# Attention with two heads stacked in the row halves of the TensorE array, maxima over two PSUM banks, one value bank, and V kept in SBUF

## The chip, the cores and the metric

The kernel runs on 1 core of one Trainium2 chip. The metric is device time in microseconds for one launch. TensorE is called PE, VectorE DVE, ScalarE ACT, GpSimd POOL and SyncE SP, as the profile does.

## The reference

Two pre-norm layers on x of shape (2, 1024, 256), fp32. Only the first step is touched by the change:

```
qkv   = layernorm(x) @ W_attn                      # 16 heads; q1,k1,q2,k2 of 8 columns a head, v of 16
attn  = q1 k1^T * scale - lam * q2 k2^T * scale    # per head, 1024 x 1024
out   = (1 - LAMBDA_INIT) * softmax(attn) @ v ;  x = x + out @ W_proj
x = x + sparse ternary MLP(layernorm(x)) ; x = x + linear attention(...) ; x = x + routed MLP(...)
```

Since q2 is scaled by -lam, a head's score is one product of contraction 16. There are 2 batches x 16 heads = 32 score matrices of 1024 x 1024.

## The kernel before, in words

Work is cut into 8 groups of G = 4 heads. Operands are split into a high fp32r part and a low rest, and a head's q and k are stacked over partitions: `qst` holds (q_hi, q_lo, q_hi), `kst` (k_hi, k_hi, k_lo), 48 rows, then two rows that hold minus the row maximum in q (high and low part) and ones in k. Rows 50 to 127 are zero in q, so that each product uses all 128 rows of the array. Each of the three ring buffers has 4 heads side by side, [128, 4, 1024].

`stage_qkv` (L157) computes q, k and v for four chunks of 512 tokens. SP writes q and k parts to DRAM (L233), v rows padded to 32 columns a head (L237), and after the second chunk loads the stack of group 0 (L244). POOL clears stacks and v buffers first. SP's instructions are in the order of the code, and the stage ends when every engine is done.

`stage_attention` (L440) has three kinds of work:
- max units (`side_unit`, L572): one 128 x 512 tile of q k^T for the maxima; 64 tiles a group, into a ring of 3 banks `ps_m`. DVE reduces each (L710), and after the last one of a group `finish_max` (L699 to L704) makes the two rows of negated maxima, which SP copies into `qst` with 8 small DMAs (L535).
- score units (`score_unit`, L592): the transposed tile k q^T with the maxima subtracted, into a ring of 3 banks `ps_s`; ACT takes the exponential (L684) into `prob`.
- value units (`value_unit`, L605): four fp32 products, one a head, each in its own 32 columns of the array, accumulate into `ps_o`, which has two banks, one for each half of the queries. The compiler makes two matmul instructions of one fp32 product, so one unit is 8 matmuls of 512 columns. After a group ACT copies `ps_o` (L691), PE transposes it (L578) and DVE divides by the sum of the exponentials (L720 to L723).

PE runs an order written out by hand: max and score alternate tile by tile, and after every 4 tiles of each there is one value unit. The maxima of group g+1 are made beside the scores of group g, with the last one 7 units (14 score tiles) ahead of the scores that need it (`LEAD`). Ahead of the first scores stands a prologue of 76 max tiles, into which the ternary weights of the MLP are worked: their sum (L614) after tile 34, their transposes (L631) at tiles 64 to 67 and 71 to 74, with L526 loading the weights, L546 to L554 on POOL, L675 on ACT. Before the stage's loads, SP waits for the writes of q, k and v (L523).

## Time and profile before

| | us |
|---|---|
| median of 3 runs (lowest, highest) | 1344.59 (1342.28, 1345.54) |
| profiled execution, span | 1344.7 |
| PE / DVE / ACT / POOL busy | 1139.2 / 921.8 / 630.1 / 231.4 |
| granted TensorE clock, mean | 0.911 of full speed |
| first max tile on PE | 89.72 |
| first exponential | 140.16 |
| first instruction of the next stage | 532.66 |

Times inside the profile are microseconds from the span's start. A group of instructions has a busy time and a mean duration of one; consecutive instructions of one engine overlap, so that the distance from start to start is shorter than the mean. Matmul ends are modelled. "Idle before" is the time the engine waited ahead of these instructions, with what ended most of it.

### The profile page before, as it was taken

The page shows a single profiled execution, that of the slowest core. Times are in us where ns is not written, and L with a number is a line of the kernel's source. Part 1 is how long each engine was busy: PE and PEld are TensorE (multiplying, and loading weights), DVE is VectorE, ACT ScalarE, POOL GpSimd, SP SyncE. Part 2 cuts the span into 40 slices and gives each one's busy share as a digit, 9 for nine tenths or more (in the row PEclk, how much of TensorE's full clock was granted, in tenths as well). Part 3 has the DMA queues.
Part 4 walks back from the last instruction along what each step waited for, and adds up shares of the span by engine and source line. Part 5 has one row for each costly group of instructions (what it writes and reads, how often), then busy time and mean ns, then how long its engine had stood idle before and what let it go on. Part 6 is the DMA issues. An engine that isn't in the chain of part 4 may idle for free. (4 is left out here: it accounts for less than half of the span.)

```text
span 1344.7 us, 16323 instructions
## 1 busy us (share of the span) xinstructions
PE 1139.2 (85%) x5920; PEld 820.3 (61%) x5920; DVE 921.8 (69%) x1953; ACT 630.1 (47%) x1106; POOL 231.4 (17%) x178
## 2 busy tenths in 40 slices
PE   0959999999999998655575747999999799999888
PEld 0834555555555533544464635888887589889786
DVE  8739888888888820458988867555554677777743
ACT  2413766676666676267664213333333433433233
POOL 9006300000000000100003322100000644744200
PEclk9965999999999999777787878999999899999859
DMA  2794422421431000000000020100000000000200
GB/s 87 213 287 66 65 33 34 64 41 26 64 39 28 1 2 32 4 1 0 1 1 1 1 82 1 48 17 32 33 16 0 32 1 1 1 1 1 83 0 4
DMA packets 34221, 48.55 MB, mean 36 GB/s; under 512 B 5310, under 2 KB 22218, under 8 KB 34122
## 3 DMA queue, kind: packets, MB, share of 16 engines
q1 hardware_dynamic: 34140, 47.51, 16.0%
q8 instruction: 47, 0.77, 0.2%
q14 instruction: 34, 0.28, 0.1%
HBM read 32.52 MB, written 14.71 MB: 35 GB/s over the span
## 5 line engine op out<-in xcount | busy, mean ns | idle before, releaser
L710 DVE TENSOR_REDUCE att_mx<-att_ps_m 128x1 f32<-128x512 f32 x512 | 316.3, 681 | 66.8 <-PE att_ps_m L572 66.8
L684 ACT ACTIVATE att_prob<-att_ps_s 128x512 f32<-128x512 f32 x512 | 267.2, 604 | 115.6 <-PE att_ps_s L592 115.5
L572 PE MATMUL att_ps_m<-kst,qst 128*128 128x512 f32 x512 | 227.5, 468 | 18.5 <-PEq L74 16.0
L592 PE MATMUL att_ps_s<-qst,kst 128*128 128x512 f32 x512 | 200.7, 404 | 4.9 <-ACT att_prob L684 4.7
L572 PEld LDWEIGHTS att_ps_m<-kst,qst 128*128 128x128 f32 x512 | 102.3, 200 | 142.2 <-DVE att_mx L710 111.0
L1719 POOL TENSOR_TENSOR qry_prod<-qry_qr,lin_ksum 128x512 f32<-128x512 f32 x64 | 87.9, 1375 | 307.3 <-ACT qry_qr L1786 307.3
L605 PE MATMUL att_ps_o<-att_prob,att_vst 128*32 128x512 f32 x1024 | 136.2, 604 | 0.0
L592 PEld LDWEIGHTS att_ps_s<-qst,kst 128*128 128x128 f32 x512 | 94.8, 188 | 42.3 <-ACT att_prob L684 27.8
L1786 ACT ACTIVATE qry_qr<-qry_ps_q 128x512 f32<-128x512 f32 x64 | 38.3, 598 | 129.8 <-PE qry_ps_q L152 116.4
L1462 DVE SCALAR_TENSOR_TENSOR key_k_lo<-key_ps_k,key_k_hi 128x512 fp32r<-128x512 f32 x64 | 44.2, 690 | 67.8 <-ACT key_k_hi L1542 67.3
L1103 ACT ACTIVATE mlp_junk<-mlp_z,mlp_nlev 128x1024 bf16<-128x1024 f32 x64 | 72.6, 1137 | 23.2 <-DVE mlp_nlev L939 21.6
L152 PE MATMUL qry_ps_o<-qry_m_hi,qry_n_hi 128*128 128x256 f32 x256 | 76.5, 299 | 0.9 <-DVE qry_n_lo L1749 0.8
L152 PE MATMUL qry_ps_o<-qry_m_lo,qry_n_hi 128*128 128x256 f32 x256 | 71.0, 277 | 0.0
L152 PE MATMUL qry_ps_o<-qry_m_hi,qry_n_lo 128*128 128x256 f32 x256 | 70.9, 277 | 0.0
L1749 DVE TENSOR_TENSOR qry_n_lo<-qry_ps_t,qry_n_hi 128x512 fp32r<-128x512 f32 x64 | 44.2, 691 | 37.3 <-ACT qry_n_hi L1775 36.9
L1542 ACT ACTIVATE key_k_hi<-key_ps_k 128x512 fp32r<-128x512 f32 x64 | 38.2, 597 | 66.0 <-PE key_ps_k L152 65.3
L829 POOL CAST mlp_wo_t<-ternary 128x2048 f32<-128x2048 bf16 x1 | 1.9, 1891 | 386.4 <-POOLq L508 386.4
L152 PE MATMUL key_ps_k<-key_w_hi,lin_xt_hi 128*128 128x512 f32 x128 | 54.2, 424 | 1.7 <-DVE lin_xt_lo L1421 1.7
L1739 DVE SCALAR_TENSOR_TENSOR qry_qn<-qry_rec,qry_qr 128x512 f32<-128x512 f32 x64 | 53.5, 836 | 2.2
L152 PE MATMUL qry_ps_q<-qry_w_hi,lin_xt_hi 128*128 128x512 f32 x128 | 51.7, 404 | 3.3 <-DVE qry_w_lo L1759 3.3
L152 PE MATMUL qry_ps_q<-qry_w_lo,lin_xt_hi 128*128 128x512 f32 x128 | 51.5, 402 | 0.0
L152 PE MATMUL key_ps_g<-key_k_hi,key_xk_hi 128*128 128x512 f32 x128 | 50.5, 395 | 0.6 <-DVE key_k_lo L1462 0.6
(348 smaller groups left out, 2395.6 us busy)
## 6 DMA issues: line engine op xcount, KB each, us to landing
qst<-qk_parts SPq DMA_DIRECT2D x24, 256.0 KB
kst<-qk_parts SPq DMA_DIRECT2D x24, 256.0 KB
qk_parts<-att_out SPq DMA_DIRECT2D x16, 256.0 KB, 3.3
qk_parts<-qkv_qk_lo SPq DMA_DIRECT2D x16, 256.0 KB, 3.4
att_vst<-v_rows SPq DMA_DIRECT2D x8, 512.0 KB
residual<-L_attn_x SPq DMA_DIRECT2D x4, 512.0 KB, 5.7
v_rows<-qkv_v_st SPq DMA_DIRECT2D x8, 256.0 KB, 5.4
v_rows<-ternary SPq DMA_DIRECT2D x8, 256.0 KB, 4.0
```

The lines of the kernel that those rows point to most:

```text
L152: ins = nc.tensor.matmul(out, a, b, start=first and n == 0, stop=last and n == len(terms) - 1)
L572: nc.tensor.matmul(ps_m[:, n % BANKS, :], qst[g % RING][:, h, t * P:(t + 1) * P], kst[g % RING][:, h, half * d.CH:(half + 1) * d.CH], star ...
L592: nc.tensor.matmul(ps_s[:, n % BANKS, :], kst[g % RING][:, h, s * P:(s + 1) * P], qst[g % RING][:, h, t * d.CH:(t + 1) * d.CH], start=True ...
L605: ins = nc.tensor.matmul(ps_o[32 * h:32 * h + 32, t, :], vst[g % RING][:, s, 32 * h:32 * h + 32], prob[:, n % RING, h, t * d.CH:(t + 1) * ...
L684: nc.scalar.activation(prob[:, s % RING, h, t * d.CH:(t + 1) * d.CH], ps_s[:, n % BANKS, :], ACT.Exp).then_inc(exp_ok, 1)
L710: nc.vector.reduce_max(mx[:, g % 2, m // NB, m % NB:m % NB + 1], ps_m[:, n % BANKS, :], AX.X)\
L1103: nc.scalar.activation(junk[:, n % 2, :], Z[:, t, :], ACT.Sign, bias=nlev[:, t:t + 1], accum_out=sgn[:, t:t + 1]).then_inc(cnt_ok, 1)
L1462: nc.vector.scalar_tensor_tensor(out=k_lo[:, i % 2, :], in0=ps_k[:, i % 2, :], scalar=0.0, in1=as_f32(k_hi[:, i % 2, :]), op0=ALU.max, op1 ...
L1719: nc.gpsimd.tensor_tensor(prod[:, u % 2, :], qr[:, u % 2, :], ksum[:, b, cols(n)], ALU.mult).then_inc(pr_ok, 1)
L1739: nc.vector.scalar_tensor_tensor(out=qn[:, u % 2, :].rearrange("p (h e) -> p h e", e=HW), in0=rec[:].unsqueeze(2).to_broadcast([P, HPB, HW ...
L1749: nc.vector.tensor_tensor(n_lo[:, u % 2, :], ps_t[:, u % 2, :], as_f32(n_hi[:, u % 2, :]), ALU.subtract).then_inc(n_ok, 1)
L1786: nc.scalar.activation(qr[:, u % 2, :], ps_q[:, u % 2, :], ACT.Relu).then_inc(q_ok, 1)
```

## The change

- `qst` and `kst` hold two heads in two row halves: head 2j in rows 0 to 49, head 2j+1 in rows 64 to 113, [128, 2, 1024]. Each product uses 50 (maxima: 48) rows of one half. Zero rows and their DRAM copy are gone; a stack is loaded with 12 DMAs in place of 7, the negated maxima with 16 in place of 8.
- The two heads' products are issued one behind the other, into two banks. A max unit is such a pair, read by one DVE reduction over two banks (`ps_m` is 2 x 2 banks). Scores are issued as pairs, into the same ring of 3 banks; one wait stands before both.
- The steps go over (group, query half t, key tile s); a step has two slots, each with a score pair, then a max pair, then one half (256 columns) of the value product of two steps earlier. `ps_o` is one bank: the values of a t start in the fourth step of it, after ACT's copy of the t before; there two slots have none, and the two after them a whole value product each.
- `prob` is a ring of 6 steps of 512 queries. V stays in SBUF (`vall`); its DRAM copy and its loads are gone.
- The prologue has 42 max pairs, the sum of weights after pair 17, the transposes at 32 to 35 and 37 to 40. The last maxima of a group stand 5 steps (10 slots) ahead of its scores.

Core of the diff (longer removed passages stand in the code above):

```diff
-                sp.wait_ge(pad_ok, 1)
-                sp.dma_start(zero_dram, as_f32(qst[0][64:66]).rearrange("r h t -> r (h t)")).then_inc(z_out, 16)
...
                     if c == d.S // d.CH - 1:
-                        sp.wait_ge(z_out, 16)
+                        sp.wait_ge(pad_ok, 2 * len(kst))
                         for i in range(d.S // d.CH):
                             sp.wait_ge(qk_out[i], 32 * NQ)
                         load_stack(d, keep, scratch, 0, sp, stack_in)
...
+                link(nc.gpsimd.memset(vall[:], 0.0))
+                nc.gpsimd.memset(vall[:, :, :, d.HD:d.HD + 1], 1.0).then_inc(v_init, 1)
+                pool.wait_ge(v_init, 1)
+                for i in range(2 * len(kst)):
+                    rows = slice(ROW2 * (i % 2) + 32, ROW2 * (i % 2) + 64)
+                    nc.gpsimd.memset(as_f32(kst[i // 2][rows, :, :]), 1.0).then_inc(pad_ok, 1)
...
-STACK_LOADS = 7
+STACK_LOADS = 12
+ROW2 = 64
...
+            src = scratch["qk"][part, b, base + h0 * d.HD:base + (h0 + d.G) * d.HD, :]\
+                .rearrange("(j r e) t -> r e j t", r=2, e=d.HD)
+            for r in range(2):
+                row = ROW2 * r + n * d.HD
+                sp.dma_start(as_f32(dst[row:row + d.HD, :, :]), src[r]).then_inc(sem, 16)
...
+        PR = 6
+        LEAD = 5
+        LAG = 2
...
-        ps_m = st.ps("ps_m", [P, BANKS, d.CH])
-        ps_o = st.ps("ps_o", [P, NB, d.CH])
-        pad_ok, gp = st.sem("pad_ok"), st.sem("gp")
+        ps_m = st.ps("ps_m", [P, 2, 2, d.CH])
+        ps_o = st.ps("ps_o", [P, d.CH])
...
+        SPG = NS * NB
+        MPG = PAIRS * NS * NB
+        STEPS = SPG * d.NG
+        NMD = 16
+        END = STEPS + LAG + 4
+        side = {u: [] for u in range(-1, END)}
         for g in range(d.NG):
             for m in range(MPG):
-                side[max(-1, UPG * (g - 1) - LEAD + m // MPU)].append(("max", g, m))
+                side[max(-1, SPG * (g - 1) - LEAD + m // PAIRS)].append(("max", g, m))
             for t in range(NB):
-                side[UPG * (g + 1) + G + 2 + t].append(("out", g, t))
-        items = [(u, x) for u in side for x in side[u]]
+                side[NS * (NB * g + t + 1) + LAG + 2].append(("out", g, t))
+        items = [x for u in side for x in side[u]]
+        values = {}
+        for u in range(STEPS):
+            for c in range(2):
+                slot = 2 * (u + LAG) + c
+                if u % NS < 2:
+                    slot = 2 * (u // NS * NS + LAG + 1) + u % NS
+                values.setdefault(slot, []).append((u, c))
...
                 def load_group(g):
...
+                    if g >= RING:
+                        sp.wait_ge(sc_ps, PAIRS * SPG * (g - RING + 1))
+                    load_stack(d, keep, scratch, g, sp, load[g % RING])
...
-                    sp.wait_ge(scratch["v_out"][i], 16 * (d.H // d.G) * d.NC // 2)
-                load_group(0)
...
+                    for n, src in enumerate((nm_hi, nm_lo)):
+                        for r in range(2):
+                            row = ROW2 * r + 3 * HD + n
+                            dst = qst[g % RING][row:row + 1, :, :].rearrange("p h (t q j) -> p (h t) q j", q=4, j=32)
+                            for q in range(4):
+                                cols = slice(32 * q + PAIRS * NS * r, 32 * q + PAIRS * NS * (r + 1))
+                                sp.dma_start(as_f32(dst[:, :, q]), as_f32(src[cols, g % 2, :]))\
+                                    .then_inc(nm_in[g % 2], 16)
...
-                pad(nc, link, keep, RING - 1).then_inc(pad_ok, 1)
...
-                    if n >= BANKS:
-                        pe.wait_ge(m_rd, n - BANKS + 1)
+                    if n >= 2:
+                        pe.wait_ge(m_rd, n - 1)
                     if kind == "max":
-                        h, t, half = m // (NS * NB), m // NB % NS, m % NB
+                        j, t, half = m // (NS * NB), m // NB % NS, m % NB
                         if m == 0 and g:
                             pe.wait_ge(load[g % RING], loaded(g))
-                        nc.tensor.matmul(ps_m[:, n % BANKS, :], qst[g % RING][:, h, t * P:(t + 1) * P],
-                                         kst[g % RING][:, h, half * d.CH:(half + 1) * d.CH],
-                                         start=True, stop=True).then_inc(m_ps, 1)
+                        for r in range(2):
+                            rows = slice(ROW2 * r, ROW2 * r + 3 * HD)
+                            ins = nc.tensor.matmul(ps_m[:, n % 2, r, :], qst[g % RING][rows, j, t * P:(t + 1) * P],
+                                                   kst[g % RING][rows, j, half * d.CH:(half + 1) * d.CH],
+                                                   start=True, stop=True)
+                        ins.then_inc(m_ps, 1)
...
+                def score_pair(u, j):
+                    g, t, s = u // SPG, u // NS % NB, u % NS
+                    n = G * u + 2 * j
+                    if u % SPG == 0 and j == 0:
                         pe.wait_ge(nm_in[g % 2], 16 * NMD * (g // 2 + 1))
-                    if n < BANKS:
+                    if n == 0:
                         pe.wait_ge(tern_rd, 2 * TB)
                     else:
...
+                        pe.wait_ge(exp_ok, n + 2 - BANKS)
+                    for r in range(2):
+                        rows = slice(ROW2 * r, ROW2 * r + 3 * HD + 2)
+                        ins = nc.tensor.matmul(ps_s[:, (n + r) % BANKS, :], kst[g % RING][rows, j, s * P:(s + 1) * P],
+                                               qst[g % RING][rows, j, t * d.CH:(t + 1) * d.CH], start=True, stop=True)
+                    ins.then_inc(sc_ps, 1)
+                def value_half(u, c):
+                    g, t, s = u // SPG, u // NS, u % NS
+                    b, h0 = g // (d.NG // d.B), g % (d.NG // d.B) * G
+                    pe.wait_ge(exp_ok, G * (u + 1))
+                    if s == 0 and c == 0 and t:
+                        pe.wait_ge(o_rd, t)
+                    if s == 0 and c:
+                        return
+                    cols = slice(c * HALF, (c + 1) * HALF) if s else slice(0, d.CH)
                     for h in range(G):
...
+                        ins = nc.tensor.matmul(ps_o[32 * h:32 * h + 32, cols], vall[:, NS * b + s, h0 + h, :],
+                                               prob[:, u % PR, h, cols], start=s == 0,
+                                               stop=s == NS - 1 and c == 1)
+                    ins.then_inc(pv_ok, 1 if s else 2)
...
-                for u in side:
+                for u in range(END):
                     todo = side[u]
-                    for t in range(NB):
+                    for j in range(PAIRS):
+                        if u < STEPS:
+                            score_pair(u, j)
                         for x in todo[:1]:
                             side_unit(*x)
-                        if u < UN:
-                            score_unit(u, t)
                         todo = todo[1:]
+                        for v in values.get(2 * u + j, []):
+                            value_half(*v)
                     for x in todo:
                         side_unit(*x)
-                    if u > G and u % G in (1, 3) and u // G - 1 < UN // G:
-                        value_unit(u // G - 1, u % G // 2)
...
+                for u in range(END):
+                    for j in range(PAIRS if u < STEPS else 0):
+                        n = G * u + 2 * j
+                        if j == 0 and u >= PR:
+                            act.wait_ge(pv_ok, 2 * (u - PR + 1))
+                        act.wait_ge(sc_ps, PAIRS * u + j + 1)
+                        for r in range(2):
+                            nc.scalar.activation(prob[:, u % PR, 2 * j + r, :], ps_s[:, (n + r) % BANKS, :],
+                                                 ACT.Exp).then_inc(exp_ok, 1)
+                    last = u - LAG - 1
+                    if last > 0 and last % NS == NS - 1:
+                        t = last // NS
+                        act.wait_ge(pv_ok, 2 * (last + 1))
+                        if t >= NB:
+                            act.wait_ge(m_rd, place("out", t // NB - 1, t % NB))
+                        nc.scalar.activation(osb[:, t % NB, :], ps_o[:], ACT.Copy).then_inc(o_rd, 1)
...
-                        nc.vector.reduce_max(mx[:, g % 2, m // NB, m % NB:m % NB + 1], ps_m[:, n % BANKS, :], AX.X)\
-                            .then_inc(m_rd, 1)
+                        nc.vector.reduce_max(mx[:, g % 2, :, m], ps_m[:, n % 2], AX.X).then_inc(m_rd, 1)
```

## Rows read from the trace of the kernel before

**Rows 1.** The page's costliest groups: xcount | busy us, mean ns | idle before, releaser.
```profile
L710 DVE TENSOR_REDUCE att_mx<-att_ps_m 128x1 f32<-128x512 f32 x512 | 316.3, 681 | 66.8 <-PE att_ps_m L572 66.8
...
L684 ACT ACTIVATE att_prob<-att_ps_s 128x512 f32<-128x512 f32 x512 | 267.2, 604 | 115.6 <-PE att_ps_s L592 115.5
...
L605 PE MATMUL att_ps_o<-att_prob,att_vst 128*32 128x512 f32 x1024 | 136.2, 604 | 0.0
```
**Rows 2.** Windows, busy us (count) by engine, granted clock, DMA share, GB/s.
```profile
140.00:486.00 346.00, 344.54 (x1811) 177.37 (x1809) 283.88 (x499) 238.36 (x462) 6.19 (x2) 1.00 0.28 39
...
74.00:90.00 16.00, 0.28 (x1) 0.31 (x2) 0.00 (x0) 0.32 (x1) 0.21 (x1) 0.62 1.06 366
```
**Rows 3.** Timeline of PE around one value unit: start us, us, instruction, count.
```profile
301.30 0.40 PE L572 MATMUL att_ps_m<-kst,qst 128*128 128x512 f32 x1
301.53 0.40 PE L592 MATMUL att_ps_s<-qst,kst 128*128 128x512 f32 x1
301.86 1.07 PE L605 MATMUL att_ps_o<-att_prob,att_vst 128*32 128x512 f32 x8
302.86 0.50 PE L572 MATMUL att_ps_m<-kst,qst 128*128 128x512 f32 x1
303.19 0.39 PE L592 MATMUL att_ps_s<-qst,kst 128*128 128x512 f32 x1
```
**Rows 4.** Timeline of SP, two groups' negated maxima and a stack load.
```profile
227.94 2.41 SPq L535 DMA_DIRECT2D qst<-att_nm_hi  x4
...
242.52 1.25 SPq L424 DMA_DIRECT2D qst<-qk_parts  x3
...
278.04 2.42 SPq L535 DMA_DIRECT2D qst<-att_nm_hi  x4
```
**Rows 5.** The page's DMA issues: KB each, us to landing.
```profile
v_rows<-qkv_v_st SPq DMA_DIRECT2D x8, 256.0 KB, 5.4
...
qst<-att_nm_hi SPq DMA_DIRECT2D x32, 4.0 KB, 1.8
```
**Rows 6.** Timeline of DVE: the prologue's first group, then a steady stretch.
```profile
90.52 38.39 DVE L710 TENSOR_REDUCE att_mx<-att_ps_m 128x1 f32<-128x512 f32 x64 [18.35 <-PE att_ps_m L572]
...
129.44 2.55 DVE L703 CAST att_nm_hi<-att_nmt 128x32 fp32r<-128x32 f32 x1
...
176.89 0.22 DVE L699 TENSOR_REDUCE att_nm<-att_mx 128x32 f32<-128x64 f32 x1
...
177.72 2.48 DVE L710 TENSOR_REDUCE att_mx<-att_ps_m 128x1 f32<-128x512 f32 x4
...
196.02 0.26 DVE L720 RECIPROCAL att_rs<-att_ps_m 128x16 f32<-128x16 f32 x1 [0.72 <-PE att_ps_m L578]
...
196.86 1.28 DVE L710 TENSOR_REDUCE att_mx<-att_ps_m 128x1 f32<-128x512 f32 x2
```
**Rows 7.** Groups by form: DVE reading 128 x 1024 fp32.
```profile
L863 DVE TENSOR_TENSOR residual<-residual,mlp_ps_t 128x1024 f32<-128x1024 f32 x3 | 3.7, 1221 | 14.4 <-PE mlp_ps_t L1183 14.4
```
**Rows 8.** Timeline of ACT and PE in the last group, where no maxima are left.
```profile
512.78 2.06 ACT L684 ACTIVATE att_prob<-att_ps_s 128x512 f32<-128x512 f32 x4 [0.61 <-PE att_ps_s L592]
...
513.43 0.50 PE L592 MATMUL att_ps_s<-qst,kst 128*128 128x512 f32 x1 [0.28 <-ACT att_prob L684]
```
**Rows 9.** Timeline, end of stage_qkv and start of the attention.
```profile
67.22 12.30 SPq L237 DMA_DIRECT2D v_rows<-qkv_v_st  x4
...
73.72 0.60 ACT L366 ACTIVATE ternary<-qkv_ps_v 128x512 f32<-128x512 f32 x1 [0.83 <-PE qkv_ps_v L152]
...
85.66 3.19 SPq L237 DMA_DIRECT2D v_rows<-ternary  x4
```
**Rows 10.** Timeline, first exponentials, and what stands after the last ones.
```profile
140.16 2.06 ACT L684 ACTIVATE att_prob<-att_ps_s 128x512 f32<-128x512 f32 x4
...
525.94 2.06 ACT L684 ACTIVATE att_prob<-att_ps_s 128x512 f32<-128x512 f32 x4 [0.54 <-PE att_ps_s L592]
...
532.66 0.40 SPq L819 DMA_DIRECT2D mlp_wp<-L_attn_W_proj  x1
```

More of the change, by code:

```diff
@@ L638, in _ @@
                         prologue[TURN_AT[i] + k] = lambda i=i, k=k: turn_weight(i, k)
-                for n, x in enumerate(side.pop(-1)):
+                for n, x in enumerate(side[-1]):
                     side_unit(*x)
@@ L676, in _ @@
                         .then_inc(tern_rd, 1)
-                for u in range(UN + G + 3):
-                    s, h = u // G, u % G
-                    if h == 0 and RING <= s < UN // G:
-                        act.wait_ge(pv_ok, NB * (s - RING + 1))
-                    for t in range(NB if u < UN else 0):
-                        n = NB * u + t
-                        act.wait_ge(sc_ps, n + 1)
-                        nc.scalar.activation(prob[:, s % RING, h, t * d.CH:(t + 1) * d.CH], ps_s[:, n % BANKS, :],
-                                             ACT.Exp).then_inc(exp_ok, 1)
-                    if u > UPG and u % UPG in (2, 4):
-                        g, t = u // UPG - 1, u % UPG // 2 - 1
-                        act.wait_ge(pv_ok, NB * (NS * (g + 1) - 1) + t + 1)
-                        if g >= 1:
-                            act.wait_ge(m_rd, ready("out", g - 1, t))
-                        nc.scalar.activation(osb[:, t, :], ps_o[:, t, :], ACT.Copy).then_inc(o_rd, 1)
+                for u in range(END):
[14 more added lines that the diff above has]
+                        nc.scalar.activation(osb[:, t % NB, :], ps_o[:], ACT.Copy).then_inc(o_rd, 1)
             @block.vector
```

121 lines of the change are left out of this document (27 added, 94 removed).

## The prediction

> **What bounds the kernel now.** I read the page's groups first, then windows over the attention, then timelines of PE, ACT, DVE and SP inside it. The two largest groups of the page are the maxima on DVE and the exponentials on ACT, and both wait for PE: 66.8 and 115.6 us idle [rows 1]. From 140 to 486 us PE is busy 344.5 of 346 us at full clock, DVE 283.9, ACT 238.4 [rows 2]. A busy PE row alone proves little, so I add up its instructions. In the stretch of 8 alternating products the distance from start to start is 301.53 - 301.30 = 0.23 us. A value unit of 8 matmuls stands between a score at 301.53 and a max product whose weight load starts at 302.86; the product after that one starts at 303.19, so the first streamed from 302.96. The unit thus costs 302.96 - 301.53 - 0.23 = 1.20 us [rows 3]. Eight products and a unit are 8 x 0.232 + 1.20 = 3.05 us, 16 of them 48.8, and two sets of transposes bring a group to the 50.1 us that lie between two sets of negated maxima, 227.94 and 278.04 [rows 4]. So PE's order of instructions is the bound, and nothing else. In the last group no maxima are left, and the exchange with ACT binds: both engines wait there for each other in turn [rows 8]. A third bound stands ahead: from 74 to 90 us PE does nothing while the DMA engines are full (share 1.06) [rows 2], because SP stood 12.30 us in the issues of v rows at 67.22, and the last ones end at 88.85, though the compute of the stage ended at 74.3 [rows 9].
>
> **The products.** A score tile and a max tile cost PE 0.232 us each. The change issues two of them in two row halves. If they stream side by side, a pair costs what one cost. The trace has no row halves; it has column quarters: the 8 matmuls of a value unit, 604 ns each [rows 1], take 1.07 us together [rows 3], so that they run as two waves of four, 1.07 - 0.60 = 0.46 us apart. Four at once with no visible loss is the nearest row. Bounds for a pair: 0.232 (full overlap) and 0.464 (none); I take 0.24.
>
> **The value halves.** A wave of 256 columns takes half of 0.45 us. A whole unit costs 1.20, of which two waves are 0.90 and the turns between the arrangements of the array, with the first weight load laid bare, 0.30. A half then costs 0.45 + 0.30 = 0.75 us. So a slot, two tiles of each kind, costs PE 0.24 + 0.24 + 0.75 = 1.23 us. Before, two tiles of each kind and half a unit cost 0.93 + 0.60 = 1.53. The turns are the change's own price: two in each slot, before two in every second one. The Trainium skill speaks of less than full overlap: its page TensorE: Matmul & The Clock Gate (Part 3, Measured speedup vs the span model) gives a speedup of 3.07 for four row tiles of 512 columns. As an estimate by that figure a pair costs 0.232 x 4 / 3.07 = 0.30, a slot 0.13 more, and the whole would be 28 us above my sum; the second rival has the same sign, and the trace of before has no row half that could tell.
>
> **DVE.** 64 reductions of 512 columns take 38.39 us, 0.600 each from start to start [rows 6]; one alone 0.681 [rows 1]. A DVE instruction over 1024 columns takes 1.221 [rows 7], 0.54 more than the 0.681. A pair's reduction then takes 0.600 + 0.533 = 1.13 us from start to start. Bounds: 1.13 and 1.22. A group has 32, 36.3 us, and finish_max 0.83 (176.89 to 177.72) and two outputs of 0.84 (196.02 to 196.86) [rows 6], 38.8 us. That is under PE's sum below, with two buffers between.
>
> **ACT and its exchange with PE.** Four exponentials take 2.06 us, so (2.06 - 0.60) / 3 = 0.49 each, a pair 0.98. But a pair of scores may start only when the first exponential of the pair before is done, since three banks hold one pair and one tile. In the last group this exchange can be read: the exponential from 512.78 ends at 513.37, the score starts at 513.43 and takes 0.50, weight load included [rows 8]; then comes the exponential. Round: 0.60 + 0.05 + 0.50 + 0.04 = 1.19 us a slot. So PE's 1.23, the exchange's 1.19 and DVE's 1.13 lie close together: PE leads by a little, and no single edit gains more by itself.
>
> **A group.** Per half of the queries, 16 slots: 12 with a value half, 12 x 1.23 = 14.8; 2 without, at the exchange's 1.20, 2.4; 2 with a whole unit, 2 x (0.48 + 1.20) = 3.4. Transposes of an output: (50.1 - 48.8) / 2, 0.6 us. ps_o is one bank now: ACT copies it behind the exponentials of a step, 0.5 us of ACT, and the first value unit of the next half waits for it, about 0.4 us; behind that unit on PE stand the next score and max pairs. Sum 21.6, 1.35 a slot, 43.2 us a group in place of 50.1. Slots with maxima reach from step 0 to 106: 214 x 1.35 = 289 us. The remaining 42 slots have no max pair; PE needs 0.99 and the exchange 1.19, with the whole units 1.24 on average: 52 us. First to last exponential 341 us, where it was 528.0 - 140.16 = 387.8 [rows 10].
>
> **The negated maxima.** SP needs 2.41 us for the issue of four, 0.60 each [rows 4]; 16 in place of 8 would be 9.6 us, and 1.8 to landing [rows 5]. Each carries half as much: bounds 0.30 and 0.60, and I take the upper, since the issue of four stack DMAs with other shapes is no cheaper per instruction (1.25 for three). From the last max pair to the scores it feeds there are 10 slots and a value half, 14.1 us; off go the reduction and finish_max, 2.5. Left 11.6 against 11.4: just hidden, with 0.3 us a group of loss, 2 us. Behind the waiting score pair on PE stands everything. Loads of stacks (12 issues of 0.42 in place of 7) have over 25 us of room: free.
>
> **The front.** Without v rows, SP issues the last q and k parts as PE makes them, until 72.5 us; the stage ends with its compute (74.3) or with the stack of group 0. 16 writes of 256 KB leave the queue (8 from each of two buffers, one of them shown [rows 5]): 4.2 MB at the 366 GB/s of 74 to 90 us [rows 2] are 11.5 us. 89.7 - 11.5 is 78.2, the compute's end gives 74.7. I put the first max at 77, bounds 75 and 87 (SP still held up in the stack's 12 issues), in place of 89.7. POOL clears less than before, when it was no wait for the first stack. From the first max: 32 pairs x 1.13 = 36.3; finish_max 3.2, since its cast stretches to 2.55 beside POOL [rows 6]; then 16 issues and landing, 11.4; in all 50.9, and a score and ACT 0.6. First exponential at 128.5 (140.16 before), 11.7 us earlier. The weights of the MLP land earlier too, and their sum and transposes stand at nearly the same tiles, so their chain is no longer than before, when it too ended a little ahead of the first exponential. PE is at half clock there (0.62 from 74 to 90 [rows 2]); scores that begin at half clock cost some 3 us, which I add.
>
> **The sum.** 128.5 + 341 + 2 + 3 = 474.5 for the end of the last exponential, 528.0 before. What stands behind it (525.94 + 2.06 to 532.66, 4.7 us [rows 10]) has the same parts. Gain 53.5; V's loads during the attention lay beside PE and give nothing. The profiled execution of 1344.7 goes to 1291. The median of the runs is 1344.6, the same within their spread, so the forecast is 1291 us.
>
> **Rivals.** (1) The halves do not stream side by side (slower than before). Place: every pair; price 0.46 in place of 0.24, a slot 0.93 + 0.75 = 1.68, 1.71 with the rest of the sum; 214 x 1.71 + 42 x 1.27 = 419 us, and with the front 1344.7 - 11.7 + 419 - 387.8 = 1364. It decides from a pair of 0.24 + 53.5 / 428 = 0.37 us on. For it: no row half is in the trace; against it: the column quarters. Chance 0.10. (2) The second half's weight load is laid bare, once a pair behind a turn: a weight load is 302.96 - 302.86 = 0.10 us [rows 3]; or DVE's two-bank reading costs 1.22 and its bursts reach PE. A slot is 0.10 to 0.13 longer, 214 x 0.12 = 26 us, 1317. That two engines lie so close speaks for it, that four column quarters load their weights together against it. Chance 0.17. (3) The negated maxima come late, each at over 0.60 beside a stack load, or the front gains nothing: 7 x 1.5 or 10 us more, 1302. Chance 0.18. (4) The turns cost less than 0.30, the copy of ps_o is never waited for, and the clock is up by the first scores: 214 x 0.06 = 13, and 5 us of the losses above, 1273. Chance 0.10. The forecast, 0.45, with its own range 1277 to 1305.
>
> **Range and chances.** The range 1265 to 1320 leaves out the first rival and the far side of the fourth. Under 0.3% (4 us) no change can be told. Faster: all but the first rival and mishaps between, 0.88; same 0.02; slower 0.10.
>
> **What would show it.** Starts of the two matmuls of a pair within some 0.01 us, and the next pair 0.24 later (first rival: 0.46 between). Value halves with two waves 0.22 apart. DVE reductions of 1.21 mean, 1.13 from start to start. From 135 to 420 us slots of 1.35 us and 43 us between sets of negated maxima; a wait of PE for the rows of negated maxima under 1 us. The first max near 77 us, with no idle stretch after 74; the first exponential near 128.5. Wrong would be: DVE or ACT busy over 95% of that stretch (then the bound is another engine), or a sum per slot over 1.45.

## The result and the profile after

Before 1343.66 us (median of 4, 1342.28 to 1345.54), after 1307.65 us (median of 4, 1307.32 to 1309.97): ratio 0.9727, 95% interval 0.9709 to 0.9745. The profiled execution has a span of 1305.6 us and a mean granted clock of 0.885, where it was 1344.7 and 0.911. The change makes the kernel faster by 36 us; forecast were 53.5. Medians are over all executions of a kernel; ratios and intervals leave out those more than 1.5% above its fastest.

The page's groups after, as in [rows 1]:
```profile
L701 DVE TENSOR_REDUCE att_mx<-att_ps_m 128x2 f32<-128x1024 f32 x256 | 303.5, 1221 | 33.1 <-PE att_ps_m L556 31.0
L673 ACT ACTIVATE att_prob<-att_ps_s 128x512 f32<-128x512 f32 x512 | 278.2, 596 | 88.0 <-PE att_ps_s L579 79.6
L595 PE MATMUL att_ps_o<-att_prob,v_rows 128*32 128x256 f32 (+1 forms) x1920 | 171.2, 439 | 5.0 <-ACT att_osb L681 4.7
```
DVE and ACT still wait for PE. A DVE reduction over two banks takes the 1221 ns that [rows 7] gave.

PE's timeline in a steady stretch after, as [rows 3]:
```profile
299.93 0.50 PE L579 MATMUL att_ps_s<-qst,kst 50*128 50x512 f32 x2
300.27 0.40 PE L556 MATMUL att_ps_m<-kst,qst 48*128 48x512 f32 x2
300.60 0.64 PE L595 MATMUL att_ps_o<-att_prob,v_rows 128*32 128x256 f32 x8
301.17 0.50 PE L579 MATMUL att_ps_s<-qst,kst 50*128 50x512 f32 x2
```
Two products (x2) last 0.40 us together, as one did; the starts of a pair are 3 ns apart. A slot is 301.17 - 299.93 = 1.24 us; predicted were 1.23. From the start of a value half to the next product it is 0.57 us, 1.00 for a whole unit in [rows 3]; a pair stands 0.33 us ahead of the value half, as one product did there. The pair of 0.30 us, the prediction's estimate from the 3.07 that the Trainium skill gives for four row tiles (TensorE: Matmul & The Clock Gate, Part 3, Measured speedup vs the span model), did not come; the span model of the same section, the duration of one product and about 4 ns for each further tile, is what these rows show for two.

Windows after, with the columns of [rows 2] (the third figure from the end is the granted clock: 1.00 is 2.4 GHz, 0.50 is 1.2):
```profile
126.00:490.00 364.00, 337.70 (x2858) 122.11 (x2860) 269.11 (x284) 277.45 (x516) 0.00 (x0) 0.92 0.17 24
237.00:240.00 3.00, 3.00 (x32) 1.21 (x28) 2.96 (x3) 2.64 (x5) 0.00 (x0) 1.00 0.00 0
240.00:243.40 3.40, 2.43 (x22) 0.96 (x20) 3.35 (x4) 3.03 (x6) 0.00 (x0) 1.00 0.00 0
243.40:247.00 3.60, 3.47 (x16) 0.82 (x14) 2.55 (x6) 1.74 (x5) 0.00 (x0) 0.53 0.01 1
```
PE is busy 338 of 364 us, no longer all the time, and the clock is 0.92. The three short windows show one place of ten: the clock rises at 134.4 us and then falls ten times before the last group begins at 445.7. In the last group it falls twice more. PE's timeline there:
```profile
240.75 0.50 PE L579 MATMUL att_ps_s<-qst,kst 50*128 50x512 f32 x2
241.09 0.40 PE L556 MATMUL att_ps_m<-kst,qst 48*128 48x512 f32 x2
242.01 0.49 PE L579 MATMUL att_ps_s<-qst,kst 50*128 50x512 f32 x2 [0.52 <-ACT att_prob L673]
242.34 0.40 PE L556 MATMUL att_ps_m<-kst,qst 48*128 48x512 f32 x2
243.19 0.51 PE L579 MATMUL att_ps_s<-qst,kst 50*128 50x512 f32 x2 [0.45 <-ACT att_prob L673]
243.54 0.59 PE L556 MATMUL att_ps_m<-kst,qst 48*128 48x512 f32 x2
244.26 1.94 PE L595 MATMUL att_ps_o<-att_prob,v_rows 128*32 128x512 f32 x8
```
The slots at 240.75 and 242.01 are the two without a value product. PE waits 0.5 us in each, and right behind them the clock falls for 3.4 us: the whole value unit takes 1.94 us, 1.07 in [rows 3]. A half is 16 slots, measured from its first exponential to that of the next half. An undisturbed one takes 22.0 to 22.1 us, one with a drop 23.2 to 23.8 (22.7 where half of the maxima are gone). Of the 13 halves behind the first, which is partly at half clock from the start, ten have a drop; the second, the fifth and the tenth have the same two slots and none.

The front after, DVE and SP (as [rows 6] and [rows 4]):
```profile
102.30 3.90 DVE L694 CAST att_nm_hi<-att_nmt 128x32 fp32r<-128x32 f32 x1
...
106.45 5.04 SPq L518 DMA_DIRECT2D qst<-att_nm_hi  x8
111.54 5.01 SPq L518 DMA_DIRECT2D qst<-att_nm_lo  x8
```
The first reduction starts at 64.6 us (90.5 before), the first exponential at 120.7 (140.16), the last exponential at 491.8, the next stage at 496.26 (532.66). The attention from the first exponential to the end of the last is 371.7 us, 387.8 before. So 19.5 of the 36.4 us up to the next stage come from the front and 16.1 from the loop (the attention from its first exponential on); predicted were 11.7 and 42 (47 less the 5 us of losses set apart).

### The profile page after: what moved, and what is told of

Same layout as the page of the kernel before. It is cut to its first block and busy times, and to the rows that moved or that the text cites. A ratio compares the mean times of both kernels' runs of the same rounds, so it can differ in the third digit from the quotient of the medians.

```text
span 1305.6 us, 18000 instructions
## 1 busy us (share of the span) xinstructions
PE 1093.7 (84%) x6816; PEld 746.8 (57%) x6816; DVE 901.1 (69%) x1697; ACT 640.8 (49%) x1106; POOL 203.4 (16%) x170
## 5 line engine op out<-in xcount | busy, mean ns | idle before, releaser
L701 DVE TENSOR_REDUCE att_mx<-att_ps_m 128x2 f32<-128x1024 f32 x256 | 303.5, 1221 | 33.1 <-PE att_ps_m L556 31.0
L673 ACT ACTIVATE att_prob<-att_ps_s 128x512 f32<-128x512 f32 x512 | 278.2, 596 | 88.0 <-PE att_ps_s L579 79.6
L595 PE MATMUL att_ps_o<-att_prob,v_rows 128*32 128x256 f32 (+1 forms) x1920 | 171.2, 439 | 5.0 <-ACT att_osb L681 4.7
L579 PE MATMUL att_ps_s<-qst,kst 50*128 50x512 f32 x512 | 133.6, 518 | 21.9 <-ACT att_prob L673 20.2
L556 PE MATMUL att_ps_m<-kst,qst 48*128 48x512 f32 x512 | 123.7, 480 | 16.7 <-DVE att_mx L701 14.4
L579 PEld LDWEIGHTS att_ps_s<-qst,kst 50*128 50x128 f32 x512 | 50.3, 192 | 145.0 <-ACT att_prob L673 128.6
L1776 ACT ACTIVATE qry_qr<-qry_ps_q 128x512 f32<-128x512 f32 x64 | 38.2, 597 | 129.9 <-PE qry_ps_q L152 116.5
L595 PEld LDWEIGHTS att_ps_o<-att_prob,v_rows 128*32 128x32 f32 x1920 | 42.0, 112 | 88.0 <-ACT att_prob L673 57.4
L1093 ACT ACTIVATE mlp_junk<-mlp_z,mlp_nlev 128x1024 bf16<-128x1024 f32 x64 | 72.6, 1137 | 23.3 <-DVE mlp_nlev L929 21.8
L556 PEld LDWEIGHTS att_ps_m<-kst,qst 48*128 48x128 f32 x512 | 54.9, 211 | 44.6 <-DVE att_mx L701 36.1
L1729 DVE SCALAR_TENSOR_TENSOR qry_qn<-qry_rec,qry_qr 128x512 f32<-128x512 f32 x64 | 53.5, 836 | 2.2
L710 DVE RECIPROCAL att_rs<-att_ps_m 128x16 f32<-128x16 f32 x16 | 4.1, 257 | 72.7 <-PE att_ps_m L563 72.7
```

The costliest lines, as they stand in the source:

```text
L556: ins = nc.tensor.matmul(ps_m[:, n % 2, r, :], qst[g % RING][rows, j, t * P:(t + 1) * P], kst[g % RING][rows, j, half * d.CH:(half + 1) * ...
L579: ins = nc.tensor.matmul(ps_s[:, (n + r) % BANKS, :], kst[g % RING][rows, j, s * P:(s + 1) * P], qst[g % RING][rows, j, t * d.CH:(t + 1) * ...
L595: ins = nc.tensor.matmul(ps_o[32 * h:32 * h + 32, cols], vall[:, NS * b + s, h0 + h, :], prob[:, u % PR, h, cols], start=s == 0, stop=s == ...
L673: nc.scalar.activation(prob[:, u % PR, 2 * j + r, :], ps_s[:, (n + r) % BANKS, :], ACT.Exp).then_inc(exp_ok, 1)
L701: nc.vector.reduce_max(mx[:, g % 2, :, m], ps_m[:, n % 2], AX.X).then_inc(m_rd, 1)
L1093: nc.scalar.activation(junk[:, n % 2, :], Z[:, t, :], ACT.Sign, bias=nlev[:, t:t + 1], accum_out=sgn[:, t:t + 1]).then_inc(cnt_ok, 1)
```

## The experiments

All ratios are to the kernel before, on the same chip. The runs were on several chips, so "less than after" compares medians or ratios, not executions side by side. Times of slots are from start to start of ACT's exponentials; "first to last" is from the first exponential to the end of the last. Traces show one execution each.

### e1_fill: does the clock fall because PE has too little to do in the thin slots?

```diff
-                        for r in range(2):
+                        for r in list(range(2)) * times:
...
-                            side_unit(*x)
+                            side_unit(*x, times=1 if values.get(2 * u + j) else 3)
```

> In the slots that have no value products, each max pair is issued three times over (the same result in the same banks). Theory: the granted clock falls to half for some 3.4 us in 11 of 13 half groups because PE is thinly used in the two slots without values; then the drops between 140 and 430 us vanish, every half group takes the 22.0 us that the undisturbed ones take now, and the whole is 15 to 20 us shorter, about 1290. The last group has no max pairs and keeps its drops: 24 and 21 us a half. Rival: the drops have another cause (the row halves themselves, or their phase is accidental); then they stay and the time is the same, or up to 3 us longer for the added products. Control: the slots 4 and 5 stay at 1.19 and 1.45 us, since PE has 0.6 us to spare in them.

1292.54 us, 0.9596 (0.9576 to 0.9615): 15 us less than after, though PE does more. (Three executions took 1290.4 to 1294.3; a fourth took 1465.0 at a mean granted clock of 0.697, and no trace shows why.) Window of e1_fill:
```profile
126.20:430.00 303.80, 295.30 (x2688) 116.69 (x2684) 266.89 (x279) 245.09 (x456) 0.00 (x0) 1.00 0.20 29
```
No drop is left in it; its halves take 21.8 to 22.3 us. From the first exponential to the last group it is 308.5 us, 325.0 in the kernel after: 16.5 less, of which 2.4 lie in the first half, where the clock rose at 126.2 us in place of 134.4, and 14.1 in the ten drops. (The expectation counts eleven.) In the last group, where no maxima are left to be repeated, the clock still falls (25.1 and 23.2 us a half), which serves as a control. So with more work for PE in the two slots the clock does not fall here. That such slots are not enough by themselves is shown by the three spared halves after, and by e4_whole_values below.

### e2_same_half: both products of a pair in one row half

```diff
-                            rows = slice(ROW2 * r, ROW2 * r + 3 * HD)
+                            rows = slice(0, 3 * HD)
```

> Both products of each pair, maxima and scores, read rows 0 to 47 (49), so both stand in the same row half; the second head's scores are then those of the first. Theory (the halves stream side by side and this is what pays): the second product starts 0.23 us after the first, a regular slot goes from 1.24 to 1.70 us, the last group's from 1.19 to 1.42, and the whole is 80 to 95 us longer, about 1390, slower than the kernel before. Rival (the gain comes from fewer, longer instructions, and the exchange with ACT hides the pair's streaming): under 25 us longer.

1685.2 us, ratio 1.253. Window, and PE's timeline, of e2_same_half:
```profile
300.00:800.00 500.00, 500.00 (x1949) 225.29 (x1949) 202.25 (x205) 187.14 (x346) 0.00 (x0) 0.50 0.09 14
```
```profile
500.00 1.22 PE L579 MATMUL att_ps_s<-qst,kst 50*128 50x512 f32 x2
501.02 1.05 PE L556 MATMUL att_ps_m<-kst,qst 48*128 48x512 f32 x2
502.00 1.08 PE L595 MATMUL att_ps_o<-att_prob,v_rows 128*32 128x256 f32 x8
```
The products now run one after the other, but the clock stays at 0.50 with PE busy all the time. That was not foreseen (expected were about 1390 us), and so the run does not give the price of overlap alone. e9_all_rows was made for that.

### e9_all_rows: the pairs use all 128 rows and cannot overlap

The rows of the other head and the padding are included in each product; the row of ones is zero and the exponential is scaled, so the values are others.

```diff
-                            rows = slice(ROW2 * r, ROW2 * r + 3 * HD)
+                            rows = slice(0, P)
```

> Every product of a pair uses all 128 rows, so the two stand one behind the other, in the same number and order of instructions; the spare rows of q are cleared first, the row of ones is zero and the exponential is scaled to nothing, so the scores are not the reference's. Theory (the row halves stream side by side, at full clock): a regular slot takes 1.70 us in place of 1.24, the clock doesn't fall since the array is used whole, a half group takes 28 to 29 us, and the whole is 75 to 95 us longer, about 1390. Rival (row halves gave little, the order and the reductions gave the most): under 30 us longer, at the kernel before or below.

1373.73 us, 1.0211 (1.0186 to 1.0236). Window and PE's timeline of e9_all_rows:
```profile
127.60:500.00 372.40, 364.79 (x2496) 182.18 (x2495) 274.79 (x279) 237.62 (x442) 0.00 (x0) 1.00 0.17 24
```
```profile
300.89 0.72 PE L582 MATMUL att_ps_s<-qst,kst 128*128 128x512 f32 x2
301.46 0.63 PE L559 MATMUL att_ps_m<-kst,qst 128*128 128x512 f32 x2
```
A pair lasts 0.63 us in place of 0.40: 0.23 more, one whole product. Slots are 1.63 and 1.75 us in turn, 1.69 on average, and a half 27.9. The whole is 65 us more than after by the ratios, less than the 75 to 95 expected; in the last group the clock falls once, for 3.4 us, where the kernel after has 13.6 us at half clock. This is the first rival in the flesh (it gave slots of 1.71 and 19 us over the kernel before; here it is 28): without overlap the change would have been slower than the kernel before.

### e3_one_bank_max: two reductions of one bank each

```diff
-                        nc.vector.reduce_max(mx[:, g % 2, :, m], ps_m[:, n % 2], AX.X).then_inc(m_rd, 1)
+                        for r in range(2):
+                            ins = nc.vector.reduce_max(mx[:, g % 2, r, m:m + 1], ps_m[:, n % 2, r, :], AX.X)
+                        ins.then_inc(m_rd, 1)
```

> Each max pair is reduced by two instructions over one bank each in place of one over two banks. Theory (PE's slot of 1.24 us covers DVE): DVE needs 1.20 in place of 1.13 us a slot, which shows only in the prologue, 42 x 0.07 = 3 us; the whole is 3 to 5 us longer. Rival (DVE is the second bound, and its share decides around the outputs): slots 8 to 10 grow too, 8 us longer or more.

1307.28 us, 0.9725 (0.9709 to 0.9742): the same as after, and not the 3 to 5 us more that were expected. DVE's reductions grow from 303.5 to 312.0 us busy, 0.03 us a pair (in the profiled execution, the longest of five with 1322.9), and PE's 1.24 covers that. Two single reductions take 0.60 us each from start to start in the prologue, 1.20 a pair for 1.13. The reduction over two banks brings nothing that can be measured here.

### e4_whole_values: both value halves in the second slot of a step

```diff
-                slot = 2 * (u + LAG) + c
+                slot = 2 * (u + LAG) + 1
```

> Both halves of a value product stand together in the second slot of a step, so that a step has one turn to the column arrangement and back in place of two. Theory (the exchange of scores and exponentials through three banks holds a slot at 1.19 us at least): the two slots of a step take 1.19 and 1.7 in place of 1.19 and 1.30, 0.4 more a step, the whole 30 to 40 us longer. Rival (PE's sum is the bound, and turns are what it pays): a step saves one turn of 0.3 us, the whole is 20 to 29 us shorter.

1333.05 us, 0.9902 (0.9886 to 0.9918), 25 us more than after (30 to 40 expected), though PE has fewer turns between arrangements. Slots are 1.19 and 1.72 us, a half 24.03. The slot without values is not faster than the exchange with ACT through three score banks allows (1.19, as predicted from [rows 8]), and the other pays for both halves. This is why the values stand in halves. Its window bears on the clock:
```profile
185.00:423.00 238.00, 197.73 (x1864) 83.57 (x1852) 203.73 (x209) 175.29 (x326) 0.00 (x0) 1.00 0.20 28
```
PE is busy only 83% of it, and the two slots without values in a row that the kernel after has stand in each half here too, with the same waits (two successive slots of 1.19 and 1.45 us); yet for nine halves in a row the clock does not fall. What decides between a half with a drop and one without is open.

### e5_v_dram: V is written to DRAM again, though nobody reads it

```diff
+                    sp.wait_ge(v_ok, 2 * (c + 1))
+                    for g in range(4):
+                        sp.dma_start(v_dram[b, g, :, t0 // P:t0 // P + d.TPC, :], ...).then_inc(v_out, 16)
...
+                sp.wait_ge(scratch["v_out"], 256)
```

> V's rows are written to DRAM too, with the 16 writes, the waits and the place among SP's instructions that they had before; nobody reads them. Everything else is as in the kernel after. Theory (these writes hold SP and the DMA engines while PE has nothing to do): the first max product stands at 77 to 80 us in place of 67.5, and the whole is 8 to 12 us longer. Rival (the earlier start comes from POOL's shorter clearing alone): 0 to 3 us longer.

1317.3 us (1314.76 and 1319.85), 0.9792: 9.7 us more. SP's timeline of e5_v_dram, as [rows 9]:
```profile
59.62 8.65 SPq L231 DMA_DIRECT2D v_rows_d<-v_rows  x4
...
74.24 3.21 SPq L231 DMA_DIRECT2D v_rows_d<-v_rows  x4
```
The first reduction moves from 64.6 to 79.2, the first exponential from 120.7 to 134.3; the whole loses less, since the loop took 368.3 us with fewer drops (371.7 after). (Where the expectations name 69.1 for the first maximum, that is the start of the fifth reduction; the first is at 64.6.) So V's writes explain 14.6 of the 26 us by which the first maximum came earlier. The rest must be something else.

### e6_pool: POOL's clearing held back

```diff
-                link(nc.gpsimd.memset(vall[:], 0.0))
+                link(nc.gpsimd.memset(vall[:, :, :, d.HD:], 0.0))
...
+                pool.wait_ge(xn_ok, 1)
```

> The kernel after, with GpSimd's clearing held back: it clears of the V tile only the columns that the V writes don't cover, and it starts on the padding of the key stacks only once the normalised input is ready. In the profile after, the four normalising operations of VectorE beside that clearing took 11.16 to 7.42 us for the same tile that takes 1.38 us undisturbed. Theory (GpSimd's clearing, not the chain itself, sets when the first q projection can start): VectorE's four operations go back to 1.4 us each, the first q projection starts at 20 to 21 us instead of 27.6, the first maximum is read 6 to 8 us earlier (61 to 63 us instead of 69.1), everything behind moves with it, and the kernel is at 1299 to 1302 us. Rival (the time is shared: what GpSimd no longer does beside the normalisation it does later, beside the projections' evictions on VectorE, and the padding becomes the last to arrive before the first stack): first maximum within 2 us of 69.1, 1306 to 1309 us.

1299.92 us, 0.9655 (0.9621 to 0.9689), 8 to 10 us less than after (by the medians and by the ratios). DVE's timeline, the same four operations in the kernel before, after and in e6_pool:
```profile
13.11 14.24 DVE L141 TENSOR_SCALAR qkv_xn<-residual,qkv_mv,qkv_rstd 128x256 f32<-128x256 f32 x4
```
```profile
11.16 7.42 DVE L141 TENSOR_SCALAR qkv_xn<-residual,qkv_mv,qkv_rstd 128x256 f32<-128x256 f32 x4
```
```profile
8.61 1.38 DVE L141 TENSOR_SCALAR qkv_xn<-residual,qkv_mv,qkv_rstd 128x256 f32<-128x256 f32 x4
```
The same work takes 14.2, 7.4 and 1.4 us. The first reduction is at 56.8 us, 7.7 earlier than after, the first exponential at 112.5. POOL's clearing of buffers slows what DVE does beside it, and everything of the front waits for the normalised input: ACT's first pass over a q projection was at 38.04 us before, 27.58 after, 19.50 here. POOL beside the normalisation, before and after:
```profile
16.47 3.54 POOL L436 MEMSET kst<- 32x4096 f32 x1
```
```profile
9.10 11.22 POOL L248 MEMSET kst<- 32x2048 f32 x6
```
Each of DVE's four operations takes as long as one clearing instruction beside it: 3.56 us for 3.54 before, 1.86 for 1.87 after. So here it was the length of POOL's single instruction that counted. The change had halved it, by stacks that are half as wide, and the 10.5 us between 38.04 and 27.58 are near the 11.4 of the front that V's writes leave open. That part is read from the traces; no run puts the old clearing back.

### e7_order: the order of a half

The copy of `ps_o` stands one step earlier, so that one slot has no value product in place of two in a row, and the third side unit of a step stands before the value half.

```diff
-                if u % NS < 2:
-                    slot = 2 * (u // NS * NS + LAG + 1) + u % NS
+                if u % NS == 0:
+                    slot = 2 * (u + LAG) + 1
...
-                        for x in todo[:1]:
+                        for x in todo[:1] if j == 0 else todo:
...
-                    last = u - LAG - 1
+                    last = u - LAG
```

> ACT copies the value bank one step earlier, behind the exponentials of the slot in which its last product stands; the first value product of a half then stands in slot 5 whole, and those of the second key tile in slots 6 and 7 in halves, so that one slot in 16 has no value product in place of two, and one has a whole product in place of two. The third side unit of a step with an output stands ahead of the value half in place of behind it. Theory (whole products behind thin slots cost 1.81 and 1.73 us, and the thin pair brings the clock down): a half group takes 21.0 to 21.4 us in place of 22.0, the drops become rarer, and the whole is 1280 to 1292. Rival (the value bank's handover then waits on ACT as long as it saves, and the clock still falls): 1300 to 1308.

1281.22 us, 0.9534 (0.9507 to 0.9561), 26 us less than after. Window of e7_order:
```profile
129.80:462.00 332.20, 313.46 (x2854) 115.03 (x2856) 265.63 (x281) 276.18 (x514) 0.00 (x0) 1.00 0.18 26
```
PE has no more to do than in the kernel after, and the clock is full throughout. Eleven of the 13 halves behind the first take 21.4 to 21.6 us (the first 23.0, two others 21.9 and 22.2), the last group 40.5, and first to last is 343.6. The profiled execution is the fastest of four (1275.6 to 1285.5); what the others lose is not traced, but their mean granted clocks are lower (0.905 down to 0.897).

The faster loop brings back a wait that the kernel after did not have. PE's timeline of e7_order, at the first scores of a group:
```profile
249.80 0.50 PE L579 MATMUL att_ps_s<-qst,kst 50*128 50x512 f32 x2 [0.71 <-DMA qst<-att_nm_lo]
```
This is the wait for the rows of negated maxima. It makes the last slot ahead of it, from score to score on PE, up to 2.0 us long in place of 1.28, some 2 us in all seven groups.

### e8_order_fill: e7_order with the spare products

The `times` edit of e1_fill, and the same products in the slots without a side unit.

> The order of e7, and spare max products, whose result nobody reads, wherever PE has room: three pairs in the slot without value products, one pair in each slot after the last maxima. Theory: no drop of the clock from the first rise to the last exponential; all 16 halves at 21.0 to 21.4 us, the last group included, and the whole is 1270 to 1278. Rival (the spare products lie on the exchange in the last group): its two halves grow to 22 us or more and eat what the clock gives back, 1280 to 1290.

1279.99 us, 0.9517 (0.9501 to 0.9533), first to last 343.4: the same as e7_order, 2 us above the range of the theory. Where no drop is left, there is nothing for the spare products to save. They cost 1 us in the last group (41.5 for 40.5) and give 1 back in the first half (22.1 for 23.0), where the clock rises at 127.1 us in place of 129.9.

### e10_order_pool: e7_order with the edit of e6_pool

> The reordered kernel (e7_order: the value copy one step earlier, 1281.2 us) with GpSimd's clearing held back as in e6_pool. Theory (the two changes lie in different stages, so their gains add): the same 6 to 8 us as in e6_pool, 1273 to 1276 us. Rival (the front's gain is not there, or comes back as a later wait of the first group's exponentials): 1279 to 1283 us.

1278.74 us, 0.9479 (0.9399 to 0.9558), its four executions 1267.6 to 1294.3. The profiled one (1272.0) has the first exponential at 112.0 and a first to last of 344.0, so the gains add where the clock holds. The mean granted clocks of the four (0.904, 0.900, 0.883, 0.878) go with their times. The median alone would not tell the theory from its rival. (The trace has no drop between 122.8 us and the last exponential; the short drops that the next expectation names lie behind the attention. Where the two slow executions lost their time is not traced.)

### e11_order_banks: four score banks, three maximum banks

```diff
-        ps_s = st.ps("ps_s", [P, BANKS, d.CH])
-        ps_m = st.ps("ps_m", [P, 2, 2, d.CH])
+        ps_s = st.ps("ps_s", [P, 4, d.CH])
+        ps_m = st.ps("ps_m", [P, 3, d.CH])
...
-                    if n >= 2:
-                        pe.wait_ge(m_rd, n - 1)
+                    if n >= 1:
+                        pe.wait_ge(m_rd, 2 * n - 1)
```

> The reordered kernel (e7_order, 1281.2 us) with the banks of PSUM dealt otherwise: four score banks instead of three, three banks for the maxima instead of two pairs, each maximum reduced from one bank by its own instruction. Theory (a slot with maxima is bound by TensorE's own sum of 1.24 us, a slot without them by the exchange of score banks with ScalarE): regular slots stay at 1.24 us and a group's half at 21.4 to 21.6 us, the last group's slots without maxima go from 1.22 to about 1.0 us, which makes that group some 6 to 8 us shorter (39.4 now), whole kernel 1272 to 1276 us. Rival (with three banks the exchange of the maxima between TensorE and VectorE, 1.13 us start to start now with two pairs, becomes what every slot waits for): slots with maxima at 1.3 to 1.4 us, halves of 22.5 us or more, 1285 to 1300 us.

1349.43 us (ten executions, 1337.93 to 1365.37), 0.9989 (0.9957 to 1.0021): by the ratios 61 us more than e7_order. Window and PE's timeline of e11_order_banks, from one of its longest executions (1363.8):
```profile
163.00:506.00 343.00, 321.80 (x2426) 119.12 (x2422) 271.74 (x464) 229.45 (x429) 0.00 (x0) 0.83 0.18 25
```
```profile
249.14 0.50 PE L557 MATMUL att_ps_m<-kst,qst 48*128 48x512 f32 x2
250.43 0.50 PE L557 MATMUL att_ps_m<-kst,qst 48*128 48x512 f32 x2 [0.79 <-DVE att_mx L703]
```
Both theories are partly right. Slots without maxima fall to 0.97 and 1.02 us, as the theory has it: there the third score bank was the bound. Slots with maxima take 1.23 and 1.35, and the slot with the third side unit 2.94 in place of 1.57, since PE waits for DVE with one maximum bank to spare; an undisturbed half is 22.9 us. That would be 1.5 us a half, some 20 in all. The larger part is the clock: between 224 and 515 us it goes to 1.2 GHz six times and stays there for 10 to 27 us, at 2.1 to 2.2 us a slot, which makes eight halves 26.5 to 33.3 us long. Five of the six falls stand right behind such a slot of 2.94 us, the sixth lies in the wait for the last group's negated maxima, 3.85 us from score to score. The whole of the run's loss is not split further.

### e12_order_fill_pool: the version the others point to

e8_order_fill with the edit of e6_pool.

> The version that the other kernels point to: the reordered kernel with GpSimd's clearing held back (e10_order_pool) and with the spare products of e8_order_fill in the slots that lack value products or maxima (they write again what the maxima read, or a bank that is not read; they change no result). e10 had its four executions at 1267.6, 1272.0, 1285.5 and 1294.3 us with mean granted clocks of 0.904, 0.900, 0.883 and 0.878; its profiled one (1272.0) has only two short drops of the clock. Theory (what is left of the spread is the clock, which still falls in some executions behind slots in which TensorE has little to do, and the spare products keep it up): the low end stays where it is, 1267 to 1272 us, and the high end goes: all executions within 1267 to 1277 us, median 1270 to 1273. Rival (the drops have nothing to do with how much TensorE has in those slots, or the spare products cost what they save): the median stays at 1275 to 1283 us with executions above 1280.

1272.59 us (5 executions, 1268.15 to 1277.86), 0.9465 (0.9441 to 0.9489): the fastest kernel of the study, 35 us under the kernel after. The high end of e10 is gone, the low end stands. One execution is 1 us above the theory's bound; it is the profiled one, and a drop of the clock is still in it, in the last group: 13.7 us from 414.8 on, a half of 26.3 us in place of 20.8 in e8_order_fill. PE's timeline right ahead of it:
```profile
413.95 0.50 PE L588 MATMUL att_ps_s<-qst,kst 50*128 50x512 f32 x2 [1.25 <-DMA qst<-att_nm_lo]
```
It stands behind the longest wait for negated maxima of this trace, a gap that the spare products do not fill; e8_order_fill has 2.25 us from score to score in the same place (2.55 here) and no drop. So the next thing to try is to hand over these maxima earlier. With four executions of e10 on one chip and five of this kernel on another, the narrowing is likely, not proven, and that the spare products made it is argued.

## Why the prediction was right, and where it was not

**Products, value halves, slot.** Right: 1.24 us a slot for 1.23, two waves of a value half 0.24 us apart for 0.22, DVE's reductions 1.13 from start to start, the exchange with ACT 1.19. (The sum for DVE uses 0.533 where its row gives 0.54; nothing hangs on it.) The first rival was wrong by its condition and near in its price (e9_all_rows: slots of 1.69 for 1.71). The second rival's extra 0.12 a slot did not come.

**The half.** 21.6 predicted, 22.0 measured when undisturbed. The term that was too small is the transposes: 0.6 us for a half. Here three slots of 1.53 stand in a row, 0.9 in all over three regular ones; the rest is 0.01 a regular slot. 14 x 0.4 = 6 us.

**The clock.** This is the step that failed. The sum had full clock after 3 us of cold start. The cold start was priced fairly: the first half took 24.4 us, 2.4 over an undisturbed one. But behind it the clock fell ten times ahead of the last group, each time behind the two slots without value products, and twice in the last group. Ahead of the last group the loop took 325.0 us, where the forecast's terms make 289 + 10 x 1.24 = 301.4. Of these 23.6 us the clock has 16.5 by e1_fill (its later rise included) and the longer half 6; some 1 is open. The last group took 46.7 us for 32 x 1.24 = 39.7; e7_order at full clock takes 40.5 there, but its order is another, so that the clock's share in these 7 us is not separated. Together 30.6, less the 5 us that the forecast had set apart for a cold clock and late maxima, are the 25.7 by which the loop was longer than forecast (371.7 for 346). The kernel without drops, e7_order, takes 343.6.

**The negated maxima.** Right in being hidden: no wait of PE for them can be seen, and they land 0.5 to 2.9 us ahead of the scores that need them. The 16 issues took 0.63 us each in the prologue and 0.66 to 0.70 in the loop, a little over the upper bound. (The bound was argued badly: a stack DMA at 1.25 / 3 = 0.42 is cheaper than 0.60, not as dear.) How close it was shows in the faster kernels, where PE does wait for them (e7_order, e12_order_fill_pool).

**The front.** Too small: 19.5 us for 11.7. V's writes were priced fairly (14.6 us at the first maximum by e5_v_dram, for 11.5 to 15). The clause that POOL clears less "when it was no wait for the first stack" looked at the wrong waiter: the clearing did not delay the stack, it slowed DVE's normalisation, the head of the stage's chain. With it the first max product came at 64.0 us for 77. Against this gain stands a prologue longer than forecast, 64.0 to 120.7 us, 56.7 for 51.5. finish_max took 4.6 us for 3.2, its cast 3.90 us beside POOL. The last transposes of the weights, at half clock, held the first score until 119.5, 1.8 us behind the landing of the maxima's rows, and ACT's table load of 1.28 us stands ahead of the first exponential.

So the misses are -7.8 us in the front, +25.7 in the loop and -0.8 behind it: the next stage starts at 496.3 us for 479.2, 17.1 late. The median is 17 above the 1291. That the time lay well inside the range is in part luck: the front's unforeseen gain took back a third of what the loop lost. The third rival's 1302 came nearer by number, but its mechanism did not happen.

## What to carry to other kernels

Two products of half the contraction in the two row halves ran at the price of one here; count the turns and the exchange of banks next, they become the bound together. When a change makes PE's work lighter, look for the slots in which it has least to do before assuming full clock: here moving work by one slot, or padding it with idle products, was worth 15 to 26 us. Where an early stage hangs on DVE, keep POOL's clearing of buffers out of that stretch, or, which no run tried, cut it into shorter instructions.

## What the runs showed of the hardware that was not expected

The granted clock does not follow PE's busy share alone. In e2_same_half PE was busy 500 of 500 us and had half clock all along, all score and max products using 48 or 50 rows of the same half; in e9_all_rows, where products also ran one after another but over 128 rows, it had full clock for 372 us; in e4_whole_values it had full clock for 238 us with PE busy 83% of them. The first two differ in the rows that a product uses, and also in the values: e9_all_rows has zeros in the spare rows and exponentials of one. Which of these made the difference is open; no run varies one of them alone.

In the kernel after two slots with 0.5 us of waiting in each were followed by a drop of 3.4 us ten times in 13 halves, and three times not; in e4_whole_values the same two slots were not, nine times in a row.

A POOL instruction beside DVE stretched a 128 x 256 operation from some 0.35 to 3.6 us (14.24 / 4), ten times, to the length of the POOL instruction itself.
